# The maxima of the first attention group taken during the projection

## What is computed

```python
x = L0_attn_x
xn = _layernorm(x, axis=-1)
x = x + _L0_attn_ref(xn, ...) + _L0_ffn_ref(xn, ...)
xn = _layernorm(x, axis=-1)
x = x + _L1_attn_ref(xn, ...) + _L1_ffn_ref(xn, ...)

# _L1_attn_ref, 16 heads of 16 channels
att = jnp.einsum('bhqd,bhkd->bhqk', q, k) * (1.0 / np.sqrt(HD))
att = att + build_alibi_bias(NH, Tx)[None]
att = jnp.where(causal[None, None], att, -jnp.inf)
att = jax.nn.softmax(att, axis=-1)
y = jnp.einsum('bhqk,bhkd->bhqd', att, v)
```

## Time and profile before

| | before |
|---|---|
| median of 3 runs | 2517.78 us (2517.63 to 2517.99) |
| the profiled execution's own time | 2520.94 us |
| its span, first to last instruction | 2519.2 us |
| PE busy | 2419.7 us (96%) |
| DVE busy | 2254.9 us (90%) |
| ACT busy | 1846.3 us (73%) |
| POOL busy | 1104.6 us (44%) |
| granted TensorE clock, mean | 0.978 |

### The profile page before, as it was taken

How to read it: one execution, slowest core, us unless ns; L and a number is a source line. 1 busy time by engine, 2 the same in 40 slices (tenths; PEclk the granted TensorE clock), 3 DMA queues, 4 the chain that set the end, 5 groups by cost and what they waited for, 6 DMA issues and landing times.

```text
span 2519.2 us, 64138 instructions
## 1 busy us (share of the span) xinstructions
PE 2419.7 (96%) x24840; PEld 1524.6 (61%) x24840; DVE 2254.9 (90%) x4278; ACT 1846.3 (73%) x3503; POOL 1104.6 (44%) x1432
## 2 busy tenths in 40 slices
PE   6779989999999799999999999999999999999998
PEld 4569989999999544545545455545454555454543
DVE  4568878888888699999999999999999999999992
ACT  2348868778777348787777787877877778778776
POOL 1145545555555214343453443544434535444344
PEclk9989999999999779999999999999999999999999
DMA  2015555555554533334244343342442443434422
GB/s 79 1 47 170 178 184 178 172 173 176 178 175 164 157 88 103 103 102 139 69 136 117 88 122 111 96 132 75 130 125 80 128 122 87 122 85 120 133 59 68
DMA packets 330088, 300.61 MB, mean 119 GB/s; under 512 B 111864, under 2 KB 280206, under 8 KB 329784
## 3 DMA queue, kind: packets, MB, share of 16 engines
q1 hardware_dynamic: 321704, 294.58, 38.7%
q10 hardware_dynamic: 8080, 1.94, 0.4%
HBM read 175.09 MB, written 118.49 MB: 117 GB/s over the span
## 4 chain that ended last, share of the span: by engine, by line
PE 52%; DVE 10%; issue 1%; ACT 1%; SPq 1%; DMA 0%; POOL 0%; POOLq 0%; ACTq 0%
PE t_y L1754 19%; PE t_a L1670 11%; PE t_r L1710 9%; PE t_r L1722 9%; DVE t_mxc L1843 8%; PE t_a L1697 4%; ACT t_prob L1782 1%; DVE t_ysw L1856 1%; DVE t_yT L1867 1%; SPq L117 0%; DVE t_rec L1860 0%; DMA t_km<-scr_k 0%; DVE t_mx L1850 0%; POOL t_res L1915 0%; SPq L104 0%
## 5 line engine op out<-in xcount | busy, mean ns | idle before, releaser
L1782 ACT ACTIVATE t_prob<-t_r 128x512 f32<-128x512 f32 (+2 forms) x2560 | 1220.7, 560 | 310.9 <-PE t_r L1722 271.3
L1843 DVE TENSOR_REDUCE t_mxc<-t_a 128x1 f32<-128x512 f32 (+3 forms) x2432 | 1430.5, 649 | 19.1 <-PE t_a L1670 15.1
L1670 PE MATMUL t_a<-t_km,t_qm 63*128 63x128 bf16 (+4 forms) x4608 | 683.9, 277 | 19.7 <-PEq L770 8.9
L1710 PE MATMUL t_r<-t_qm,t_km 51*128 51x512 bf16 (+3 forms) x3072 | 628.0, 326 | 4.2 <-ACT t_prob L1782 0.7
L1754 PE MATMUL t_y<-t_prob,t_v 128*32 128x512 f32 (+3 forms) x6144 | 627.9, 496 | 0.9 <-POOL t_prob L1920 0.9
L1722 PE MATMUL t_r<-t_q,t_k 58*128 58x128 bf16 (+4 forms) x4608 | 614.2, 270 | 0.0
L1670 PEld LDWEIGHTS t_a<-t_km,t_qm 51*128 51x128 bf16 (+1 forms) x4608 | 273.9, 94 | 536.3 <-DVE t_mxc L1843 426.8
L1920 POOL TENSOR_SCALAR_AFFINE_SELECT t_prob<-t_prob 128x512 f32<-128x512 f32 x512 | 323.9, 634 | 610.5 <-ACT t_prob L1782 608.9
L1722 PEld LDWEIGHTS t_r<-t_q,t_k 51*128 51x128 bf16 (+1 forms) x4608 | 323.0, 94 | 41.2 <-issue 0.3
L1710 PEld LDWEIGHTS t_r<-t_qm,t_km 51*128 51x128 bf16 x3072 | 234.7, 94 | 89.0 <-ACT t_prob L1782 60.3
L1754 PEld LDWEIGHTS t_y<-t_prob,t_v 128*32 128x32 f32 x6144 | 134.3, 108 | 165.9 <-issue 95.1
(11 more groups left out here) (209 smaller groups left out, 3788.5 us busy)
## 6 DMA issues: line engine op xcount, KB each, us to landing
scr_q<-j_part SPq DMA_DIRECT2D x96, 256.0 KB, 3.4
scr_k<-j_part SPq DMA_DIRECT2D x96, 256.0 KB, 2.6
t_qm<-scr_q SPq DMA_DIRECT2D x384, 64.0 KB
t_km<-scr_k SPq DMA_DIRECT2D x384, 64.0 KB
t_q<-scr_q SPq DMA_DIRECT2D x384, 64.0 KB
t_k<-scr_k SPq DMA_DIRECT2D x384, 64.0 KB
scr_v<-j_v SPq DMA_DIRECT2D x32, 544.0 KB, 5.0
t_v<-scr_v SPq DMA_DIRECT2D x64, 272.0 KB
```

The source lines that it names most:

```text
L1670: mm = pe.matmul(abank[n % A_SLOTS][:, at + lo:at + hi], q_main[z][part, h, i * P:(i + 1) * P], k_main[z][part, h, k0 + lo:k0 + hi], start ...
L1710: pe.matmul(ring[n % RING_BANKS][:, at * w:(at + 1) * w], k_main[z][part, heads[at], j * P:(j + 1) * P], q_main[z][part, heads[at], q0:q0 ...
L1782: nc.scalar.activation(prob[:, q % SLOTS, h0:h0 + m, 0:w], ring[n % RING_BANKS][:, 0:m * w].rearrange("p (h n) -> p h n", h=m), ACT.Exp).t ...
L1843: V.tensor_reduce(out, data, AX.X, ALU.max, negate=True).then_inc(s_au, 1)
```

## The change

The 38 units of group 0 are done in project, as 19 double units: one for both pairs of heads in `b_turn0`, 512 columns each, at steps 12 to 30. On PE a unit stands between `f0` and `q`; on DVE its reduction, of up to 1024 columns, stands between `x1` and `mix0`. `turn0` two steps later waits for that reduction. `mxc` is now set by POOL at the start of project. SP loads what the maxima of group 1 need (20 DMAs) in `first_group` too, which now has 59 DMAs and comes after step 3's ffn store, and no longer at the start of attend. In attend, group 0's 38 units are gone, and its `join` comes first on DVE.

```diff
-        N_SET = 3
+        N_SET = 4
...
                 load_marks(sp, a, scr, qm0, km0, s_qk0)
+                load_marks(sp, a, scr, qm1, km1, s_qk1)
                 load_constants(sp, a, scr, q0, k0, s_qkv0)
...
                 for e in range(2):
                     load_maxima(sp, a, scr, qm0, km0, 0, s_qk0, e)
+                for e in range(2):
+                    load_maxima(sp, a, scr, qm1, km1, 1, s_qk1, e)
...
-                    if m == 6:
+                    if m == 3:
                         first_group()
...
+            def first_maxima(u):
+
+                pieces, two = MAX_UNITS[u]
+                if u == 0:
+                    pe.wait_ge(s_qk0, 16 * (MARKS + MAX_LOADS))
+                at = 0
+                for h in two:
+                    for i, k0, w, near in pieces:
+                        far = w - P if near else w
+                        for depth, lo, hi in ((NMAIN, 0, far), (NMAX, far, w)):
+                            if lo < hi:
+                                for e in range(2):
+                                    part = slice(HALF * e, HALF * e + depth)
+                                    mm = pe.matmul(b_turn0[:, 512 * e + at + lo:512 * e + at + hi],
+                                                   qm0[part, h, i * P:(i + 1) * P], km0[part, h, k0 + lo:k0 + hi],
+                                                   start=True, stop=True)
+                        at += w
+                mm.then_inc(s_first_pe, 1)
...
-            for what, m in cycle([("turn1", 0), ("kv", -1), ("f0", 1), ("q", 0), ("k", 0), ("kk", 0), ("v", 0),
+            for what, m in cycle([("turn1", 0), ("kv", -1), ("f0", 1), ("max", 0), ("q", 0), ("k", 0), ("kk", 0), ("v", 0),
                                   ("turn0", 2), ("r", 0)]):
                 if what == "turn0":
...
+                    if m - 2 >= FIRST_AT:
+                        pe.wait_ge(s_first, min(m - 2 - FIRST_AT + 1, len(MAX_UNITS)))
...
+            def first_maxima(u):
...
+                dve.wait_ge(s_first_pe, u + 1)
...
+                V.tensor_reduce(out, data, AX.X, ALU.max, negate=True).then_inc(s_first, 1)
...
-                                  ("mix0", -2), ("mix_low1", -2), ("rest_q", -2), ("stats1", -1), ("mix_low0", -2),
+                                  ("max", -2), ("mix0", -2), ("mix_low1", -2), ("rest_q", -2), ("stats1", -1), ("mix_low0", -2),
...
+            pool.memset(mxc[:, :, :, :], 3.0e38).then_inc(s_set, 1)
...
+FIRST_AT = 12
...
+    pl.done.update({("max", 0, u): 0.0 for u in range(NU)})
...
+    maxima_in(0)
     for rank, kind, t, x in cyclic():
+        if kind == "max" and t == 0:
+            continue
...
             sp.dma_start(identb[:, :], a["identb"]).then_inc(s_id, 16)
-            first_keys(1)
             first_load(1)
             first_keys(2)
             first_keys(3)
...
-                dve.wait_ge(s_au, used[last_max(t)])
+                if t == 0:
+                    dve.wait_ge(s_first, len(MAX_UNITS))
+                else:
+                    dve.wait_ge(s_au, used[last_max(t)])
...
-            V.memset(mxc[:, :, :, :], 3.0e38)
```

More of the change, by code:

```diff
@@ L150, in prepare @@
         keep(early, "t_km0", [P, GH // 2, T], BF16)
+        keep(early, "t_qm1", [P, GH // 2, T], BF16)
+        keep(early, "t_km1", [P, GH // 2, T], BF16)
+        keep(early, "t_mxc", [P, 2, GH, 2 * QT])
         blocks = keep(early, "t_blocks", [KM - KB, P])
@@ L153, in prepare @@
         markb = [keep(early, f"t_mark{n}", [MSUB, P], BF16) for n in "qk"]
-        for name in ("t_s_qkv0", "t_s_qk0"):
+        for name in ("t_s_qkv0", "t_s_qk0", "t_s_qk1", "t_s_first"):
             scr[name] = early.enter_context(nc.semaphore(name))
@@ L782, in project @@
         q0, k0, v0, qm0, km0 = (scr["t_" + n] for n in ("q0", "k0", "v0", "qm0", "km0"))
-        s_qkv0, s_qk0 = scr["t_s_qkv0"], scr["t_s_qk0"]
+        qm1, km1, mxc = scr["t_qm1"], scr["t_km1"], scr["t_mxc"]
+        s_qkv0, s_qk0, s_qk1, s_first = (scr["t_s_" + n] for n in ("qkv0", "qk0", "qk1", "first"))
         scr["ffn"] = nc.dram_tensor("scr_ffn", (B, T, D), FP32, kind="Internal").ap()
@@ L830, in project @@
         s_link, s_xbias = sem("j_dve_link"), sem("j_xbias")
+        s_first_pe = sem("j_first_max_pe")
         xt = a["x"].rearrange("b (h t p) c -> (b h) p t c", p=P, t=TPM)
@@ L941, in _ @@
                     by_token(b_f0, xT, w["w0"]).then_inc(s_f0, 1)
+                elif what == "max":
+                    if 0 <= m - FIRST_AT < len(MAX_UNITS):
+                        first_maxima(m - FIRST_AT)
                 elif what == "turn1":
@@ L1088, in remainder @@
                 i.then_inc(s_rest[n], 1)
+            def first_maxima(u):
+                pieces, two = MAX_UNITS[u]
+                i, k0, w, near = pieces[0]
+                to = QT * k0 // 512 + i
+                dve.wait_ge(s_first_pe, u + 1)
+                if u == 0:
+                    dve.wait_ge(s_set, N_SET)
+                mine = mxc[:, 0, :, :]
+                if len(two) == 2:
+                    out = mine[:, :, to:to + QT + 5:QT + 4]
+                    data = b_turn0[:, :].rearrange("p (h s n) -> p h s n", h=GH, s=2)
+                elif len(pieces) == 2:
+                    out = mine[:, two[0]:GH:2, to:to + QT + 5:QT + 4]
+                    data = b_turn0[:, :].rearrange("p (e s n) -> p e s n", e=2, s=2)
+                else:
+                    out = mine[:, two[0]:GH:2, to]
+                    data = b_turn0[:, :].rearrange("p (e n) -> p e n", e=2)[:, :, 0:w]
+                V.tensor_reduce(out, data, AX.X, ALU.max, negate=True).then_inc(s_first, 1)
             for what, m in cycle([("stats0", 0), ("xT_low", -1), ("x1_low", -2), ("ffn", -3), ("mix1", -2), ("x1", -1),
-                                  ("mix0", -2), ("mix_low1", -2), ("rest_q", -2), ("stats1", -1), ("mix_low0", -2),
+                                  ("max", -2), ("mix0", -2), ("mix_low1", -2), ("rest_q", -2), ("stats1", -1), ("mix_low0", -2),
                                   ("rest_k", -2), ("vbias", -2), ("ksq_low", -2)]):
@@ L1509, in attend @@
         k_rest = [scr["t_k0"]] + [sb(f"t_k{n}", [P, GH // 2, T], BF16) for n in range(1, BUFS)]
-        q_main = [scr["t_qm0"]] + [sb(f"t_qm{n}", [P, GH // 2, T], BF16) for n in range(1, MAIN_BUFS)]
-        k_main = [scr["t_km0"]] + [sb(f"t_km{n}", [P, GH // 2, T], BF16) for n in range(1, MAIN_BUFS)]
+        q_main = [scr["t_qm0"], scr["t_qm1"]] + [sb(f"t_qm{n}", [P, GH // 2, T], BF16) for n in range(2, MAIN_BUFS)]
+        k_main = [scr["t_km0"], scr["t_km1"]] + [sb(f"t_km{n}", [P, GH // 2, T], BF16) for n in range(2, MAIN_BUFS)]
         v = [scr["t_v0"]] + [sb(f"t_v{n}", [P, QT, VPAD], FP32) for n in range(1, BUFS)]
         prob = sb("t_prob", [P, SLOTS, GH, 512])
-        mxc = sb("t_mxc", [P, 2, GH, 2 * QT])
+        mxc = scr["t_mxc"]
         mx = sb("t_mx", [P, 2, GH, QT])
@@ L1534, in attend @@
         s_qkv = [scr["t_s_qkv0"]] + [sem(f"t_qkv_in{n}") for n in range(1, BUFS)]
-        s_qk = [scr["t_s_qk0"]] + [sem(f"t_qk_main_in{n}") for n in range(1, MAIN_BUFS)]
+        s_qk = [scr["t_s_qk0"], scr["t_s_qk1"]] + [sem(f"t_qk_main_in{n}") for n in range(2, MAIN_BUFS)]
+        s_first = scr["t_s_first"]
         s_a = sem("t_a_pe")
@@ L1555, in attend @@
         slot = {e: n for n, e in enumerate(in_slot)}
-        first_max = [min(slot["max", t, u] for u in range(NU)) for t in range(GROUPS)]
+        first_max = [None] + [min(slot["max", t, u] for u in range(NU)) for t in range(1, GROUPS)]
         used = [sum(e[0] != "rows" for e in in_slot[:n + 1]) for n in range(len(in_slot))]
```

## The result

| | before | after |
|---|---|---|
| median of 20 runs, us | 2518.30 | 2521.61 |
| lowest to highest | 2515.03 to 2521.64 | 2519.68 to 2525.36 |
| profiled execution, us (span) | 2520.94 (2519.2) | 2519.74 (2518.0) |
| busy in the profile, us: PE / DVE | 2419.7 / 2254.9 | 2398.2 / 2253.0 |

The ratio is 1.0014, 95% interval 1.0008 to 1.0020: the change costs about 3.3 us (2 to 5). That is a difference from no change at all, and it lies within the 0.2%.

The account below looks back on a forecast made before the run. PE was taken to bound the projection, PE and DVE steady attend, DVE alone attend's start. Attend's start -13.0, burst +10.6 and units +8.3 sum to +5.9 on the median 2517.78: 2523.7 us, range 2514.5 to 2530.

Parts of the forecast that it names:

- The start of attend: DVE at attend's start: group 0's reductions gone, but a longer wait for group 2's operands; 13.0 us earlier, bounds 12 to 14.
- The burst of loads: SP's queue in the projection: 20 added DMAs delay q's store, a pure shift of +10.6 us, 10 to 12.
- Moving the burst from step 6 to step 3 is worth nothing: SP's loads in the projection: the move costs nothing, since both steps lie in the steady stretch.
- Units on PE: PE in the projection: 19 units at 0.44 us, columns plus two changes of tiling, 8.3 us; bounds 3.9 to 12.3.
- up to another 0.1: PE behind a unit: extra us in the change to the whole array, from the second full matmul starting 0.22 behind the first.
- DVE's reduction at nothing: DVE in the projection: each unit's reduction costs nothing, covered by 1.56 us of idle time in each step.
- Rival 2: Projection burst: the added issue is hidden, q's store goes out within 25 us; sum -5.2, 2512.6 us; chance 0.10.
- within: Whole kernel: outcome class of a change within 0.2%, 5.0 us; chance 0.32, from rival 1.
- slower: Whole kernel: outcome class of slower by over 0.2%; chance 0.58, from the forecast and rivals 3 and 4.
- The first rival: Whole kernel, also rival 1: terms stand but sum within 5 us (unit 0.3, burst 9); +1.7, 2519.5 us; chance 0.32.
- the forecast: Whole kernel: the main case, all terms as told, sum +5.9, 2523.7 us; chance 0.42.

Follow-up runs that it names:

- e4: The changed kernel with group 2's maxima operands loaded ahead of group 1's remaining ones at the start of attend; 2515.96 us, ratio 0.9985 to the changed kernel.
- e3: The changed kernel with group 1's maxima operands loaded at the start of attend again, leaving 39 loads behind step 3; 2528.18 us in one execution.
- e10: The kernel before, with its burst of 39 loads behind step 5's ffn store instead of step 6's; two steps took 51.81 us.
- e7: The kernel before, with its burst of 39 loads behind step 3's ffn store instead of step 6's; 2519.03 us in one execution.
- e5: The changed kernel with each unit's matmuls issued twice on PE before its one reduction; 21.99 us a step, 2526.37 us in one execution.
- e9: The changed kernel with a unit's matmuls all on one half of the array first, then all on the other; 21.73 us a step.
- e6b: The changed kernel with each of the nineteen DVE reductions done twice, once into a tile nobody reads; 21.94 us a step, 2529.01 us in one execution.
- e1: The changed kernel with its 59 loads issued six at a time behind each store of q from step 4 on; 2503.67 us, ratio 0.9939 to before.

## Why the prediction was right or wrong

- **The start of attend, -13.0**: right. -12.9, with a wait of 13.88 us for the 13.7, for the reason given: group 2's operands stand behind group 1's remaining ones in SP's queue. e4 and e3 change only that order and move the wait to 4.58 and to 12.59 + 11.67.
- **The burst of loads, +10.6**: the mechanism right, the term too large by 1.0; it measured +9.6, below the bound of 10 that was given to it. What was mis-sized is "10.6 us more before `q`'s store". The added issues took 10.4 us, but the burst's own six loads of `t_q` took 2.75 us instead of 4.06, so q's stores were only 9.15 us later, and their landing added 0.4: ACT waited 9.5 us longer, PE 9.7. I took the rest of the burst as fixed from one reading of it. Each of the four bursts of 39 loads has one row that is 0.7 to 1.3 us longer than its like (4.06 us for six loads in before, 3.87 for six in e10, 1.92 and 2.37 for three in e7 and e3, where the others take 2.75 and 1.25); the five bursts of 59 have none. Why is open. The sentence that every compute engine already stands still when q's store goes out is wrong in one point: PE worked until 366.3 us, 2.8 behind the store's issue. It changed nothing, since PE then waited 6.6 us.
- **"Moving the burst from step 6 to step 3 is worth nothing"**: right in ACT's wait (11.1 in both, e7), wrong in the whole: two executions (e7, e3) lose 1.3 us more at step 3, from the clock's later rise behind the stall. At that step the twenty loads cost 8.2 and not 9.6. The prediction priced no clock in this term; with 59 loads the stretch at 0.50 was as long as in before, so the sum didn't suffer. That is luck.
- **Units on PE, 0.44 each, +8.3**: 0.406, +7.7. The split is right in kind, columns of two halves side by side (e5: 0.26 for a second set), plus two changes. These cost 0.15 to 0.2, where the prediction had 0.19 to 0.29: the "up to another 0.1" of the first full matmul was counted at half. It shows in `q`'s matmuls as 0.07, and the streams behind give it back. The Trainium skill's "TensorEngine Tiling (Array Packing)", section "Key Properties", says that a change of the tiling mode drains TensorE. e5 is in line with it, since matmuls added without a change cost less than the unit's first set; no run shows the drain itself. Issue in turn, which the reasoning didn't need but which I believed, does nothing (e9).
- **DVE's reduction at nothing**: right; e6b shows how much cover was left.
- **Rival 2, a burst hidden**: fell. q's store went out 34.4 us behind the ffn store, not within 25, and e1, with the same transfers issued six at a time, won 17.9 us against after. The Trainium skill, "DMA: Bandwidth & Descriptors", section "Issuing engines are not separate DMA queues", says that the time to start a DMA "is usually small relative to the DMA itself". These runs don't contradict that for a single DMA: one issue takes 0.3 to 0.95 us, and 2.3 us pass from the end of the last one to the first reduction with the data. But it doesn't bound the sum of many on one queue, 10.4 us for twenty, and that is what the prediction asked of it.
- **The sign and the class.** The terms I forecast sum to +5.9; they came as -12.9 + 9.6 + 7.7 = +4.4, and the medians say +3.3. Both small errors had the same direction, and with the rest of attend at -0.7 the result fell 1.7 us under the 5.0 that part "within" from "slower". The first rival is right in the size of the sum; its two reasons came halfway (a burst of 9.6, where it had 9 and the forecast 10.6) or hardly (a unit of 0.41, where it had 0.3 and the forecast 0.44). Its doubt that `q`'s 512 columns would make the change cheaper didn't come true: the change in front costs the same 0.09, and 0.07 show in `q`. I gave the forecast 0.42 with a sum that stood only 0.9 above this limit, though the bounds of its terms spread from 0 to +12: a chance near that of rival 1 would have been fair. Two things that no term held could have moved the time as far as the terms did: the clock's part at the burst (1.3 us) and `prepare` (up to 5 us in a single execution). That the time came within 2.1 us of 2523.7 is in part luck.

## What to carry to other kernels

A change that moves work out of a stage where one engine is alone pays what its operands' loads cost where they now stand, and what its visits cost on the full engine: add up both before asking how many microseconds come off. When a queue issues dozens of small DMAs in one go ahead of a store that frees a buffer, spread them a few a step behind that store; here this was worth 8.7 us in the kernel before and 17.9 in the changed one, more than the change itself could bring. And when work ahead of a chain is taken away, look at what the next link waits for: nineteen steps of work ahead of time gained 2.4 us at the start of attend without the next operands, 12.9 with one group of them, and 26.9 with two.

## What the runs showed of the hardware

- **The same code took from 132.5 to 137.5 us** from the start to the projection's first load: 132.5 to 132.9 in four executions, whose mean granted clock in the window from 20 to 40 us was 1.00, and 134.7 to 137.5 in eight, where it was 0.78 to 0.91. The difference of up to 5 us is as large as the effect that was to be measured, and it falls out only when stages are compared from marks of their own.
- **A stall costs more than its wait.** Behind the same wait of ACT, 11.1 us, PE worked for 3.5 us (before) or 6.1 us (e7) at the clock of 0.50 before 1.00 was granted, about 1.6 or 2.7 us of loss by the distances between matmuls at either clock. Behind the wait of 20.6 us it was 3.2 to 3.5 us in five executions, so the longer stall had no longer stretch. What decides is open.
- **Row-tiled matmuls on the two halves overlapped just as well when all of one half were issued first** (e9, 21.73 us a step in both orders; a unit of 512 columns for each half takes 0.34 us to the next stream's start, less than the 0.43 of 1024 columns at 2.4 GHz).
- **The issue time of the same loads varies.** Six loads of `t_q` or `t_k` held SP's queue for 2.75 us in most groups and for 4.06 (before) or 3.87 (e10) in others. Each of four bursts of 39 loads had one such longer row, none of five bursts of 59 had one.
- **First pair to end varied from 1610.7 to 1613.0 us** over the kernels, with the same instructions in all of them and no relation to the edit. Its cause was not found, and effects of 1 us or so on the total are not settled by these runs.
